# Scan of a state-space layer: the router's normalised rows by ScalarE instead of GpSimd, and their bias by VectorE

## The reference

```
x = x + mamba(layernorm(x))
x = x + ffn(layernorm(x))          # its router: logits = layernorm(x) @ gate_w
x = x + attn(layernorm(x))
x = x + ffn(layernorm(x))

def step(h, inp):                  # the scan, per token; 16 states per channel
    h = dA_t * h + dBu_t
    y_t = einsum('bis,bs->bi', h, C_t)

def layernorm(x): return (x - mean(x)) / sqrt(var(x) + 1e-5)
```

## Time and profile before

| | |
|---|---|
| time, median of 3 runs | 1245.97 us (1245.11 to 1248.42) |
| the profiled execution's own time | 1244.75 us |
| its span | 1242.9 us |
| mean granted TensorE clock | 0.942 |
| busy: TensorE, VectorE, ScalarE, GpSimd | 1050.2, 907.7, 840.1, 540.3 us |
| the scan: first and last `L956` start | 143.3 and 507.2 us |

### The profile page before, as it was taken

How to read it: one execution, slowest core, us unless ns; L and a number is a source line. 1 busy time by engine, 2 the same in 40 slices (tenths; PEclk the granted TensorE clock), 3 DMA queues, 4 the chain that set the end, 5 groups by cost and what they waited for, 6 DMA issues and landing times. The chain is left out here.

```text
span 1242.9 us, 24539 instructions
## 1 busy us (share of the span) xinstructions
PE 1050.2 (84%) x7470; PEld 755.6 (61%) x7470; DVE 907.7 (73%) x1967; ACT 840.1 (68%) x1736; POOL 540.3 (43%) x363
## 2 busy tenths in 40 slices
PE   2875499988888888769949999989999999992897
PEld 1442388888888888549934454545454555551897
DVE  7697789989889889546635686857685867673565
ACT  4897599988888889346625666747574757571564
POOL 0389588999999999524420001010101010011344
PEclk9898599999999999889978999999998999995899
DMA  3000244434674664133311000000000000001331
GB/s 91 4 2 4 88 114 132 126 120 124 195 209 125 179 191 123 53 93 98 111 43 35 1 2 18 1 19 1 18 0 19 1 18 9 10 18 56 96 92 47
DMA packets 84425, 83.40 MB, mean 67 GB/s; under 512 B 23735, under 2 KB 62396, under 8 KB 84320
## 3 DMA queue, kind: packets, MB, share of 16 engines
q1 hardware_dynamic: 75440, 60.20, 17.9%
q0 software_dynamic: 5568, 12.66, 2.9%
q10 hardware_dynamic: 3312, 9.33, 2.5%
HBM read 65.73 MB, written 17.35 MB: 67 GB/s over the span
## 5 line engine op out<-in xcount | busy, mean ns | idle before, releaser
L956 DVE TENSOR_TENSOR_SCAN h<-d_a,p_dbu 128x1024 f32<-128x1024 f32 x128 | 289.0, 2278 | 33.1 <-ACT d_a L735 24.0
L686 POOL TENSOR_TENSOR h<-h,c_rep 128x1024 f32<-128x1024 f32 x126 | 294.7, 2371 | 18.5 <-DVE h L956 16.5
L1896 ACT ACTIVATE arena<-arena,at_min 128x512 f32<-128x512 f32 x256 | 183.3, 720 | 120.5 <-DVE at_min L2007 118.2
L2007 DVE CUSTOM_DVE_ANT_0 arena<-at_p_scores,arena 128x512 f32<-128x512 f32 x256 | 174.5, 685 | 84.5 <-PE at_p_scores L1771 48.3
L1257 POOL TENSOR_SCALAR r_row<-r_row 128x4 f32<-128x4 f32 x16 | 3.7, 234 | 472.2 <-DVEq L1162 472.2
L735 ACT ACTIVATE d_a<-arena,a_exp 128x511 f32<-128x511 f32 x256 | 169.3, 710 | 16.5 <-DVE h L956 16.4
L1778 PEld LDWEIGHTS at_p_probs_T<-ident,arena 128*128 128x128 f32 x1024 | 113.1, 142 | 95.6 <-issue 69.5
L1771 PE MATMUL at_p_scores<-arena,at_q_T 64*128 64x512 f32 x512 | 162.2, 649 | 7.1 <-DVE at_min L2007 5.4
L727 ACT ACTIVATE b_du_T<-arena,b_T 128x256 f32<-128x256 f32 x392 | 166.0, 495 | 0.1
L1778 PE MATMUL at_p_probs_T<-ident,arena 128*128 128x128 f32 x1024 | 159.0, 284 | 4.0 <-ACT arena L1896 2.3
L856 PE MATMUL p_y_T<-ident,h 128*128 128x128 f32 x1024 | 133.5, 273 | 5.8 <-POOL h L686 5.7
(11 more groups left out here) (244 smaller groups left out, 1604.3 us busy)
## 6 DMA issues: line engine op xcount, KB each, us to landing
c_rep<-c_rows SPq DMA_DIRECT2D x128, 256.0 KB, 3.7
f_row<-expert_rows SPq DMA_DIRECT2D x78, 129.0 KB
diag_b<-diag_rows SPq DMA_DIRECT2D x30, 256.0 KB, 4.1
arena<-in_w_all ACTq DMA_DIRECT2D x8, 578.0 KB, 4.6
arena<-bias_by_distance ACTq DMA_DIRECT2D x8, 448.0 KB, 4.4
x_tok<-in_x SPq DMA_DIRECT2D x4, 512.0 KB, 4.9
x_tok<-x_between SPq DMA_DIRECT2D x8, 256.0 KB, 2.8
diag_rows<-diag_b SPq DMA_DIRECT2D x4, 256.0 KB, 5.2
```

What stands on the lines that cost most here:

```text
L686: nc.gpsimd.tensor_tensor(h[:, n % HS, :, :], h[:, n % HS, :, :], cc, ALU.mult).then_inc(prod_done, 1)
L956: nc.vector.tensor_tensor_scan(h[:, n % HS, :, :].rearrange("p c t -> p (c t)"), da[:, s % 2, :, :].rearrange("p c t -> p (c t)"), p_dbu[: ...
L1896: nc.scalar.activation(pr[:, slot, :], sc[:, slot, :], ACT.Exp, scale=-1.0, bias=mn[:, slot:slot + 1]).then_inc(probs_ready, 1)
L2007: V.tensor_tensor_reduce(sc[:, slot, :], psc[:, s % SCB, :], band[:, hd, w0:w0 + T], 1.0, 3.0e38, ALU.add, ALU.min, mn[:, slot:slot + 1]). ...
```

## The change

The four row operations leave GpSimd's stream. ScalarE writes the rows instead, behind the exponentials of state 11 (`act_normed`): `Identity` with a scale and a bias per token, x * rstd + shift. The bias, shift = -mean * rstd, is one VectorE operation on 128x4 numbers behind the scan of state 9 (stage 3 of `dve`), written into the unused `veps`. The wait on the landed send moves with the rows to ScalarE. This concerns the batches 1 to 7 of the scan (the rows of sequences 0 to 6); the last sequence's rows and the second mixture's router stay as they were.

```
             # GpSimd, batch(b)
-                    if s == 10 and b > 0:
-                        rt.pool_rows(pool, b - 1)
             # ScalarE, batch(b, number)
                     exps(b, s)
+                    if number > 0 and s == 11:
+                        rt.act_normed(act, b - 1)
             # VectorE
-            EARLY = {0: 8, 1: 8, 4: 14, 5: 15}
+            EARLY = {0: 8, 1: 8, 3: 9, 4: 14, 5: 15}
...
+            self.shift, self.shift_ready = self.veps, S("shift_ready")
...
+        elif stage == 3 and self.in_psum:
+            dve.wait_ge(self.rstd_ready, 1 + b)
+            V.scalar_tensor_tensor(out=self.shift, in0=self.mv[:, :, 0], scalar=-1.0, in1=self.rstd,
+                                   op0=ALU.mult, op1=ALU.mult).then_inc(self.shift_ready, 1)
...
+    def act_normed(self, act, b):
+        act.wait_ge(self.shift_ready, 1 + b)
+        self.rows_out(act, b)
+        for j in range(TPB):
+            ins = self.k.nc.scalar.activation(self.row[:, j, 0:D], self.k.x[:, b * TPB + j, :], ACT.Identity,
+                                              scale=self.rstd[:, j:j + 1], bias=self.shift[:, j:j + 1])
+        ins.then_inc(self.ln_ready, 1)
...
-    def pool_rows(self, pool, b):
-        pool.wait_ge(self.rstd_ready, 1 + b + self.rstd_from)
-        self.rows_out(pool, b)
-        for j in range(TPB):
-            ins = self.k.nc.gpsimd.tensor_scalar(self.row[:, j, 0:D], self.k.x[:, b * TPB + j, :], self.mv[:, j, 0:1],
-                                                 self.rstd[:, j:j + 1], ALU.subtract, ALU.mult)
-        ins.then_inc(self.ln_ready, 1)
```

## The result

The kernel after takes **1273.34 us** (median of 4 runs, 1270.55 to 1275.05) against 1245.54 us of the kernel before on the same chip (4 runs, 1243.26 to 1248.42): a ratio of 1.0221, 95% interval 1.0196 to 1.0246. The forecast was 1247.0 us, its range ended at 1253.0. The change makes the kernel 2.2% slower.

What follows compares the result with a forecast made beforehand. GpSimd's and ScalarE's limits were taken to lie close together in states 11 to 15; added rows and landing waits less removed waits made +1.05 us on 1244.75, so 1245.8, a median of 1247.0 us, range 1241.5 to 1253.

Steps and rivals of the forecast that it cites:

- the price of the bias: VectorE's bias, beside GpSimd's product of state 7, waits for that product's end: 1.1 us per batch, bounds 0.1 and 2.5.
- the text's own signs of being wrong: Bias over 1.4 us, ScalarE pausing in quiet batches 3 and 5, or a period below 45.5 us.
- Slower: the bias waits for two products, not one: Rival: bias 2.33 us later, ScalarE held 2.15 us in six batches; +8.8, giving 1256 us; chance 0.08.
- The cover: ScalarE reaches its rows at 353.40, after the bias, so its wait is hidden; beyond that each us is paid in full.
- The rows on ScalarE: Four row operations behind state 11's exponentials cost ScalarE 1.55 us per batch, bounds 1.5 to 1.7.
- The waits removed and the period: ScalarE's 0.90 us and VectorE's 1.22 us late in a batch vanish; period falls from 46.70 to 46.1 us.
- some 2 us a batch: Sign expected: with its rows gone, GpSimd idles some 2 us per batch ahead of its products.
- The landing waits: ScalarE waits ahead of its rows for the last send to land: 1.2, 0, 1.7, 0, 0.3, 0.9 us, batches 2 to 7.
- The 1.2 us between the last packet and the landing: Added to each send's last packet time, from one send: landing 2.96 us behind the issue's end less 1.8.
- Behind it the last products, the gate and all later stages follow scan 15 as before: After scan 15 of batch 7, everything later in the kernel was to keep its distance, with no change in time.
- the forecast's sum of +1.05 us: Shifts of scan 15 over batches 1 to 7: +1.55, +0.3, -0.6, +1.1, -0.6, -0.3, -0.4.

Runs made afterwards that it cites:

- e2: Kernel after, with GpSimd waiting for its own previous product ahead of the products of states 8 and 9: 1241.44 us, ratio 0.9964 to the kernel before.
- e12: Kernel after, with a tiny GpSimd operation and a wait for its completion between the send and the product of state 7: 1239.56 us.
- e10: Kernel after, with GpSimd held up in batch 1 alone: its product of state 7 waits until the scan of state 8 is done: 1272.29 us.
- e5: Kernel after, but the rows back on GpSimd, in state 8, and the bias, not read, behind the scan of state 10: 1253.63 us.
- e6: e2 with GpSimd's pause ahead of the product of state 9 only: 1255.55 us, ratio 1.0063 to the kernel before.
- e4: Kernel after without the bias operation; the mean stands in, so the rows are wrong: 1241.71 us, ratio 0.997 to the kernel before.
- e14: e12 timed beside the kernel before: 1242.5 us, ratio 0.9963.
- e7: e2 with the rows shared, two tiles by ScalarE in state 11, two by GpSimd in state 10: 1240.99 us, ratio 0.9947 to the kernel before.
- e15: e7 with the one pause of e12 behind the send in place of its two: 1240.38 us, ratio 0.9947 to the kernel before.
- e9: Kernel after, with the bias two places later, behind the scan of state 10: 1285.1 us.
- e11: Kernel after, with the bias behind the second input copy and GpSimd waiting for the scan of state 9 behind the send: 1249.9 us.
- e13: e12 without the wait, the tiny operation running directly into the product of state 7: 1274.32 us.

## Why the prediction was wrong, point by point

**The step that failed is the price of the bias.** The text took 1.1 us with "0.1 us and a whole product, 2.5" as bounds, from the earlier trace rows, where VectorE got in at the first end of a GpSimd operation. It measured 5.65, outside the bounds, and the text's own signs of being wrong came: a bias over 1.4 us, and pauses of ScalarE in the batches 3 and 5 (3.88 and 4.21 us). What was overlooked is in the earlier trace rows itself: there GpSimd's second operation reads what the first wrote and waits for its completion, so there is a pause at that end. In batch 4 there is none from the send on the earlier trace rows. With a pause put there, the number is right: in batch 4 1.02 us in e2, 1.17 in e12. The Trainium skill's rule (page "SBUF — State Buffer", section "SBUF: two separate sides": the port pair is held for the whole instruction) gave the same 1.1 us. The trace agrees where GpSimd paused (0.93 us in e10, up to the end of the running product), and differs behind the send, where three whole products passed, and in e5, where a row operation didn't hold the bias to its end.

**The rival with the right mechanism was too short and too unlikely.** "Slower: the bias waits for two products, not one" had the place and the way of the loss, at 8 in 100. Two products would have meant 3.4 us, which e6 made on purpose: 1255.55 us, against 1256 worked out. That these agree is partly luck: the rival added 8.8 us to a forecast of 1247.0, while e6 lies 14.1 above e2's 1241.44. In the change it was three, and nothing in the argument limited them to two: the bound of a wait for a free moment is the whole row of work that is ready, here until GpSimd itself needs VectorE.

**The cover was as stated, with more behind it.** "If the cover went (a bias ready after 353.40), each further us would be paid in full": the pauses in six batches are 25.9 us, and the scan got 28.6 longer. Per quiet batch the pause of 4.2 us is most of the 5.2 by which 51.2 exceeds the 46.0 of e2 and e4; the 0.52 us at the turned rows is another part, and the last 0.4 I didn't trace.

**The rows on ScalarE**: 1.55 us forecast, 1.65 us for four with the overlap, 477 to 494 ns each. In batch 1, where nothing else acts, the maximum of the rows comes 1.6 us later (228.05 against 226.44).

**The waits removed and the period.** Forecast 46.1 us; 46.04 us in e4 and 46.02 in e2. ScalarE's 0.90 us and VectorE's 1.22 us are gone there. GpSimd stands idle instead, as forecast some 2 us a batch: in e4 0.80 us for a scan and, by the profile, 1.76 us for the transfer of a C tile (`c_rep`), which the text didn't have.

**The landing waits were sized too high.** The forecast was 1.2, 0, 1.7, 0, 0.3 and 0.9 us, 4.1 in all; e4 shows 1.2 in all, 0.72 in batch 2 and 0.44 in batch 4:

```profile
353.03 0.49 ACT L1195 ACTIVATE r_row<-x_tok,r_mv,r_rstd 128x128 f32<-128x128 f32 x1 [0.44 <-DMA expert_rows<-r_row,r_dest]
```

The 1.2 us between the last packet and the landing, taken from one send, was the term that was too large: in both batches of e4 the last packet came 2.6 us behind the last issue's end, and ScalarE's wait ended 0.6 us after that. Waits differ between runs; in e14 the two are 0.86 and 0.76 us.

**"Behind it the last products, the gate and all later stages follow scan 15 as before"** was off by 1.6 us in these versions: from the maximum of batch 7 to that of the last sequence it was 23.98 us before, and 22.35 to 22.44 in e2 and e4. GpSimd's last row of products ended 4.5 us behind the maximum of batch 7 (505.72) before, and 1.3 us behind it (503.98) in e2:

```profile
500.90 9.29 POOL L686 TENSOR_TENSOR h<-h,c_rep 128x1024 f32<-128x1024 f32 x4
```

```profile
493.58 11.67 POOL L686 TENSOR_TENSOR h<-h,c_rep 128x1024 f32<-128x1024 f32 x5
```

(the kernel before, then e2). In e7 and e15, which keep half of the rows on GpSimd, this stretch is 23.4 and 23.1 us. That GpSimd's end is the cause isn't shown: in the kernel after its last product ends at 534.65, ahead of the maximum at 535.30, and the stretch is 23.54 us.

So without the hold of the bias the forecast's sum of +1.05 us comes out at -0.9 to +0.5 (e2, e4, e12, e14, from the first scan to the maximum of batch 7, 362.4 us before), and its end adds -1.6. The measured gain of e2, e4 and e14 is some 4 us. The other 2 us or so lie outside the scan and are not explained: the start of the first scan alone lies between 142.0 and 145.6 us in the profiled executions of these kernels, whose code up to there is the same.

## What to carry to other kernels

A small VectorE operation with two inputs in SBUF, beside GpSimd operations with two inputs in SBUF, had no fixed price here: behind a send and without a pause it cost what GpSimd still had ready. Take the upper bound for it from GpSimd's whole row of ready work and not from one instruction. Put one input in PSUM, or give GpSimd a real pause behind its transfers; either made the 28 us loss a small gain here. And when a price is taken from another place in the trace, look whether the neighbours wait for each other there.

## What the hardware showed that I had not expected

- Behind a send of GpSimd (four indirect transfers) that runs into products without a pause, VectorE's two-input operation was not let in at any end of a product while another was ready: 5.65 us, to the end of the third product, in the kernel after and 5.16 us, to the end of the fourth, in e9. Behind a pause it got in at the first end (0.93 us in e10, 1.96 in e11). A pause of 0.09 us was enough (e12); a small operation without one wasn't (e13).
- GpSimd's row operations, which read one tensor from SBUF, hardly kept it out: 0.14 us in the middle of one, 0.26 to 0.40 us in three batches, never to the operation's end (e5).
